# A decoder kernel: values copied out of PSUM by ScalarE, their biases folded into the output bias, and the self blocks' rotated keys and queries rounded by ScalarE

## The reference, cut to what matters

```python
Q = (x @ wq.T + bq); K = (x @ wk.T + bk); V = (x @ wv.T + bv)   # split into 16 heads
Q, K = _rope(Q, K)                                             # only in layer 0's self attention
out = softmax(Q @ K.T / sqrt(8)) @ V                           # by head, then joined
x = layernorm(x + out @ wo.T + bo)
```

## Time and profile before

| | us |
|---|---|
| median of 3 runs | 429.88 (429.31 to 430.05) |
| the profiled execution's own time | 428.95 |
| its span on the core | 427.0 |
| PE busy | 382.7 (90%) |
| DVE busy | 282.6 (66%) |
| ACT busy | 226.1 (53%) |

### The profile page before, as it was taken

How to read it: one execution, slowest core, us unless ns; L and a number is a source line. 1 busy time by engine, 2 the same in 40 slices (tenths; PEclk the granted TensorE clock), 3 DMA queues, 4 the chain that set the end, 5 groups by cost and what they waited for, 6 DMA issues and landing times.

```text
span 427.0 us, 9206 instructions
## 1 busy us (share of the span) xinstructions
PE 382.7 (90%) x3326; PEld 337.5 (79%) x3326; DVE 282.6 (66%) x833; ACT 226.1 (53%) x526; POOL 53.8 (13%) x61
## 2 busy tenths in 40 slices
PE   4679898998989999999978999899999969989991
PEld 3577776886779997989967899778998757768991
DVE  6598889888965557622786355754768688835453
ACT  2145566665665564766347555585465546641241
POOL 7700004900000000000000000000002002010124
PEclk9989999999999999999969999999999989999997
DMA  5655311214240000200020000200011112730301
GB/s 161 192 165 182 112 48 29 74 53 119 94 136 2 2 2 0 76 2 2 2 74 2 2 0 2 67 10 1 2 39 51 38 38 72 226 124 2 110 13 33
DMA packets 22603, 25.15 MB, mean 59 GB/s; under 512 B 3224, under 2 KB 17313, under 8 KB 22560
## 3 DMA queue, kind: packets, MB, share of 16 engines
q1 hardware_dynamic: 21088, 22.95, 18.3%
q0 software_dynamic: 512, 0.97, 0.7%
q10 hardware_dynamic: 960, 0.66, 0.6%
HBM read 17.82 MB, written 6.83 MB: 58 GB/s over the span
## 4 chain that ended last, share of the span: by engine, by line
PE 70%; DVE 18%; issue 5%; DMA 3%; ACT 2%; POOL 0%; SPq 0%; POOLq 0%; ACTq 0%; DVEq 0%
PE bank_D L839 13%; PE bank_C L725 10%; PE bank_D L697 9%; PE bank_A L708 8%; DVE negmax L1225 5%; PE bank_A L855 4%; PE bank_A L857 3%; PE bank_A L856 3%; PE bank_D L623 2%; PE bank_D L681 2%; DVE x_rows L1170 1%; PE bank_D L756 1%; PE bank_A L643 1%; PE bank_A L1540 1%; PE bank_A L767 1%
## 5 line engine op out<-in xcount | busy, mean ns | idle before, releaser
L1225 DVE TENSOR_REDUCE negmax<-bank_D 128x2 f32<-128x512 f32 x192 | 127.4, 684 | 42.2 <-PE bank_D L697 41.9
L985 ACT ACTIVATE expo<-bank_A 128x512 f32<-128x512 f32 x192 | 110.2, 597 | 50.5 <-PE bank_A L708 49.2
L697 PE MATMUL bank_D<-k_head,q_sp 128*128 128x256 f32 x384 | 91.1, 322 | 9.8 <-DVE negmax L1225 5.1
L708 PE MATMUL bank_A<-q_sp,k_head 128*128 128x256 f32 x384 | 82.5, 300 | 4.8 <-DVE q_sp L1220 3.4
L1021 ACT ACTIVATE hidden<-bank_A,b 128x256 f32<-128x256 f32 x128 | 53.7, 471 | 52.1 <-PE bank_A L857 51.9
L697 PEld LDWEIGHTS bank_D<-k_head,q_sp 128*128 128x128 f32 x384 | 61.7, 199 | 22.1 <-issue 10.1
L839 PE MATMUL bank_D<-mix_w,hidden 128*128 128x128 f32 x512 | 67.8, 275 | 0.0
L708 PEld LDWEIGHTS bank_A<-q_sp,k_head 128*128 128x128 f32 x384 | 60.8, 194 | 7.6 <-DVE q_sp L1220 5.0
L839 PEld LDWEIGHTS bank_D<-mix_w,hidden 128*128 128x128 f32 x512 | 62.5, 191 | 1.6 <-issue 1.6
L725 PE MATMUL bank_C<-expo,v_aug 128*32 128x256 f32 x768 | 46.4, 382 | 1.1 <-ACT expo L985 0.8
L1284 DVE SCALAR_TENSOR_TENSOR y_mixture<-bank_D,g_w,y_mixture 128x128 f32<-128x128 f32 x64 | 22.3, 348 | 30.5 <-PE bank_D L839 28.8
(11 more groups left out here) (181 smaller groups left out, 536.4 us busy)
## 6 DMA issues: line engine op xcount, KB each, us to landing
mix_w<-in_mix_w SPq DMA_DIRECT2D x24, 256.0 KB, 3.6
k_head<-k_scratch SPq DMA_DIRECT2D x92, 48.0 KB
k_scratch<-qk_hi SPq DMA_DIRECT2D x24, 128.0 KB, 2.4
w_last<-in_mix_w SPq DMA_DIRECT2D x8, 256.0 KB, 5.7
k_scratch<-qk_lo SPq DMA_DIRECT2D x12, 128.0 KB, 2.4
proj_w<-in_proj SPq DMA_DIRECT2D x1, 640.0 KB, 5.1
xe_scratch<-empty_row SPq DMA_DIRECT2D x1, 520.0 KB, 4.5
expo<-xe_scratch SPq DMA_DIRECT2D x2, 260.0 KB, 3.1
```

The lines of the kernel that those rows point to most:

```text
L697: last = mm(where(seq, b, ("max", k))[:, qt * SEQ:(qt + 1) * SEQ], q_sps[SET[seq, b]][:, k // 4, qt * P:(qt + 1) * P], k_heads[SET[seq, b] ...
L708: last = mm(where(seq, b, ("exp", h))[:, kt * SEQ:(kt + 1) * SEQ], k_heads[SET[seq, b]][:, t, g, kt * P:(kt + 1) * P], q_sps[SET[seq, b]][ ...
L985: activate(expo[:, exp_slot(seq, b, h), :], where(seq, b, ("exp", h))[:], ACT.Exp, scale=float(HD) ** -0.5).then_inc(free(seq, b, ("exp", ...
L1225: V.tensor_reduce(negmaxes[SET[seq, b]][:, s // 4, :, 32 * (s % 4)], where(seq, b, ("max", s))[:].rearrange("p (q n) -> p q n", q=QT), AX. ...
```

## The change

The values' PSUM bank moves from pool D to pool A, and ACT copies the values out by two plain copies, without a bias, in all twelve blocks. The biases of V in layer 0 are folded: in sequence 0's self and cross block PE turns the bias row (step 6, pool A), ACT copies it to `bias_T`, PE multiplies it with the output weights (step 9, pool D), and DVE adds the product to the output bias's row in place. POOL's residual waits until that is done. In self blocks DVE adds the rotated parts (steps -13 and -5), ACT rounds the sum to `qk_hi` in the same steps, and DVE subtracts one step later (-12 and -4).

```diff
-KEYS_AT, KEYS_LOW_AT = -14, -13
-QUERIES_AT, QUERIES_LOW_AT, QUERIES_SPREAD_AT = -6, -5, -3
+KEYS_AT, KEYS_LOW_AT, SELF_KEYS_LOW_AT = -14, -13, -12
+QUERIES_AT, QUERIES_LOW_AT, SELF_QUERIES_LOW_AT, QUERIES_SPREAD_AT = -6, -5, -4, -3
 OWN_VALUES_AT = -4
+FOLD_TURN_AT, FOLD_AT = 6, 9
+FOLDED = {SELF0: ("bv0", "bo0"), CROSS0: ("bvx0", "box0")}
...
             if s == OWN_VALUES_AT:
-                turn(seq, b, "v", "D")
+                turn(seq, b, "v", "A")
+            if s == FOLD_TURN_AT and seq == 0 and b in FOLDED:
+                turn(seq, b, "bias", "A")
+            if s == FOLD_AT and seq == 0 and b in FOLDED:
+                turn(seq, b, "fold", "D")
...
                 def residual(seq, b, bias):
+                    if b in FOLDED:
+                        wait_drained(pool, 0, b, "fold")
...
+                        if s == FOLD_TURN_AT and seq == 0 and b in FOLDED:
...
+                            nc.tensor.transpose(where(seq, b, "bias")[:, 0:P], row(FOLDED[b][0]), ident
+                                                ).then_inc(full(seq, b, "bias"), 1)
+                        if s == FOLD_AT and seq == 0 and b in FOLDED:
+                            wait_drained(pe, seq, b, "bias")
+                            wait_free(pe, seq, b, "fold")
+                            mm(where(seq, b, "fold")[:, 0:P], bias_T[:], weight(wo[b]),
+                               start=True, stop=True).then_inc(full(seq, b, "fold"), 1)
...
+                def round_rotated(seq, b, i, added, ready):
+
+                    act.wait_ge(added, seq + 1)
+                    activate(qk_hi[:, i, :], rope[:, 0, :], ACT.Copy).then_inc(ready, 1)
...
+                def values(seq, b):
+
+                    if (seq, b) in BEFORE:
+                        prior, block_before = BEFORE[seq, b]
+                        act.wait_ge(pair_done, 2 * ORDER[prior, block_before] + 2)
...
+                    wait_filled(act, seq, b, "v")
...
+                        last = activate(v_column(v_augs[SET[seq, b]], odd, 0, HD), src, ACT.Copy)
+                    last.then_inc(free(seq, b, "v"), 1)
...
                 def split(seq, b, what, i, ready):
 
-                    wait_drained(dve, seq, b, what)
-                    link(V.tensor_tensor(rope[:, 0, :], rope[:, 0, :], rope[:, 1, :], ALU.add))
-                    rounded = V.tensor_copy(qk_hi[:, i, :], rope[:, 0, :])
                     if what == "k":
-                        rounded.then_inc(k_high_ready, 1)
                         dve.wait_ge(k_high_ready, seq + 1)
                     else:
-                        link(rounded)
+                        dve.wait_ge(q_high_ready, seq + 1)
                     V.tensor_tensor(qk_lo[:, i, :], rope[:, 0, :], qk_hi[:, i, :].bitcast(f32),
                                     ALU.subtract).then_inc(ready[seq], 1)
```

More of the change, by code:

```diff
@@ L955, in copy_out @@
                              ).then_inc(free(seq, b, what), 1)
+                def values(seq, b):
+                    if (seq, b) in BEFORE:
+                        prior, block_before = BEFORE[seq, b]
+                        act.wait_ge(pair_done, 2 * ORDER[prior, block_before] + 2)
+                    else:
+                        act.wait_ge(dve_cleared, 4 * SETS + 1)
+                    wait_filled(act, seq, b, "v")
+                    for odd in range(2):
+                        src = where(seq, b, "v")[:, 0:QT * P].rearrange(
+                            "p (q a b d) -> p q a b d", q=QT, b=2, d=HD)[:, :, :, odd, :]
+                        last = activate(v_column(v_augs[SET[seq, b]], odd, 0, HD), src, ACT.Copy)
+                    last.then_inc(free(seq, b, "v"), 1)
                 bk = {CROSS0: col("bkx0"), CROSS1: 0.0}
@@ L961, in attention @@
                     for s in ATTENTION_STEPS:
+                        if s == OWN_VALUES_AT:
+                            values(seq, b)
+                        if s == FOLD_TURN_AT and seq == 0 and b in FOLDED:
+                            wait_filled(act, seq, b, "bias")
+                            activate(bias_T[:], where(seq, b, "bias")[:, 0:P], ACT.Copy
+                                     ).then_inc(free(seq, b, "bias"), 1)
                         if s == KEYS_AT and b > SELF0:
@@ L964, in attention @@
                             high(seq, b, "k", 1, bk[b])
+                        if s == KEYS_LOW_AT and b == SELF0:
+                            if (seq, b) in NEXT_TO:
+                                act.wait_ge(k_stored, 16 * KEY_KINDS * ORDER[seq, b])
+                            round_rotated(seq, b, 1, k_added, k_high_ready)
+                        if s == QUERIES_LOW_AT and b == SELF0:
+                            round_rotated(seq, b, 0, q_added, q_high_ready)
                         if s == QUERIES_AT and b > SELF0:
@@ L1086, in _ @@
                 V = nc.vector
-                def values(seq, b, bv):
-                    if b == SELF0:
-                        dve.wait_ge(ld_bv0, 16)
-                    elif bv is not None:
-                        dve.wait_ge(ld_rows, 16)
-                    if (seq, b) in BEFORE:
-                        prior, block_before = BEFORE[seq, b]
-                        dve.wait_ge(pair_done, 2 * ORDER[prior, block_before] + 2)
-                    wait_filled(dve, seq, b, "v")
-                    for odd in range(2):
-                        src = where(seq, b, "v")[:, 0:QT * P].rearrange(
-                            "p (q a b d) -> p q a b d", q=QT, b=2, d=HD)[:, :, :, odd, :]
-                        dst = v_column(v_augs[SET[seq, b]], odd, 0, HD)
-                        if bv is None:
-                            last = V.tensor_copy(dst, src)
-                        else:
-                            bias = row(bv).rearrange("p (a b d) -> p a b d", b=2, d=HD)[:, :, odd, :]
-                            last = V.tensor_tensor(
-                                dst, src, bias.unsqueeze(1).broadcast_to([P, QT, HEADS // 2, HD]), ALU.add)
-                    last.then_inc(free(seq, b, "v"), 1)
                 def low(seq, b, what, i, bias):
@@ L1184, in attention @@
                             rotate(seq, b, "k", "bk0", "bk0s")
-                        if s == KEYS_LOW_AT:
+                        if s == KEYS_LOW_AT and b == SELF0:
+                            add_rotated(seq, b, "k", k_added)
+                        if s == (SELF_KEYS_LOW_AT if b == SELF0 else KEYS_LOW_AT):
                             if (seq, b) in NEXT_TO:
@@ L1191, in attention @@
                                 low(seq, b, "k", 1, bk[b])
-                        if s == OWN_VALUES_AT:
-                            values(seq, b, bv[b])
+                        if s == FOLD_AT and seq == 0 and b in FOLDED:
+                            wait_filled(dve, seq, b, "fold")
+                            dve.wait_ge(ld_rows, 16)
+                            V.tensor_tensor(row(FOLDED[b][1]), where(seq, b, "fold")[:, 0:P],
+                                            row(FOLDED[b][1]), ALU.add
+                                            ).then_inc(free(seq, b, "fold"), 1)
                         if s == QUERIES_AT and b == SELF0:
@@ L1196, in attention @@
                             rotate(seq, b, "q", "bq0", "bq0s")
-                        if s == QUERIES_LOW_AT:
+                        if s == QUERIES_LOW_AT and b == SELF0:
+                            add_rotated(seq, b, "q", q_added)
+                        if s == (SELF_QUERIES_LOW_AT if b == SELF0 else QUERIES_LOW_AT):
                             if b == SELF0:
```

10 lines of the change are left out of this document (9 added, 1 removed).

## The result

The changed kernel takes 432.56 us (median of 8 runs, 431.67 to 435.86), the kernel before 429.44 (8 runs). The ratio is 1.0076, 95% interval 1.0055 to 1.0098: slower by 2.4 to 4.2 us, where no change was forecast (430.3 us, 427.7 to 432.5). The profiled execution took 432.37 us, of which 430.2 are the span.

The account below looks back on a forecast made before the run. PE was taken to bound 120 to 210 us, with PE and DVE near each other from 26 to 120. Terms summed to +0.4 us on the profiled 428.95, giving 429.35, or 430.3 as median; range 427.7 to 432.5 (8 in 10).

Parts of the forecast that it names:

- the term for the PE-bound stretches: Stretches with a mixture beside the attention: nothing, ACT's bursts at worst making PE wait once or twice, +0.1 us (0 to +0.8).
- Start and block 1's keys: First key loads 0.65 us later behind ACT's rounding, 0.67 saved in block 1's key step, first fold 0.28: +0.25 us.
- Query steps of blocks 2 and 5: aT held behind ACT's rounding, product by key 1.0 us late, spread behind the exponential: +0.35 us each.
- Key steps: Blocks 2 and 5: first bank some 0.7 us earlier, but ACT's second exponential held behind the rounding: -0.25 us each.
- Values in cross blocks: Blocks 3 and 4: without the values' turn in pool D the scores start 0.2 us sooner: -0.2 us each.
- Work moved: DVE loses 24 value instructions (6.7 us) and 8 casts (2.7), gains two fold additions: 8.9 us off; ACT gains some 9.
- Sum: All terms: 0.25 + 0.1 + 0.7 - 0.5 - 0.4 + 0.1 + 0.15 (second fold) = +0.4 us.
- ACT's queue becomes the bound: Six later rounding copies wait for DVE ahead of work PE needs: +2.25 us, 432.1 us; chance 0.28.
- DVE's relief reaches the end: From 26 to 120 us DVE loses some 4.0 us, half of it gained: 427.9 us; chance 0.31.
- The clock: New waits at blocks 2 and 5 let the granted clock fall, 1.5 us or so each: 433.3 us; chance 0.08.
- what I said would show it: New profile: rounding behind DVE's addition, PE waits by product by key, longer DVE waits, later loads, short value copies.
- the two signs that I had given for a wrong forecast: PE's waits for DVE in 26 to 120 us shrink by 2 us unreplaced, or waits for ACT grow in mixture stretches.

Follow-up runs that it names:

- experiment 1: Run v_in_d: the changed kernel with the values' turn taken from pool D again, ScalarE still copying them; 430.96 us against 429.83, ratio 1.0029.
- experiment 5: The kernel before with only the values' turn moved from pool D to pool A, DVE still copying them; 434.06 us against 429.20, ratio 1.0104.
- v_in_d: The changed kernel with the values' turn back in pool D, ScalarE still copying; 430.96 us (ratio 1.0029), in a second set 429.49 (0.9994).
- experiments 1, 4, 6: 1: v_in_d. 4: round_only and round_only_first. 6: the changed kernel with ScalarE rounding the self blocks' queries one step later, behind the aT copy; 431.75 us, ratio 1.0055.
- experiment 2: The changed kernel with DVE rounding the self blocks' keys and queries again, values still on ScalarE in pool A, folds kept; 431.66 us, ratio 1.0052.
- round_only: The kernel before with only the self blocks' rounding on ScalarE, DVE's value copies ahead of its subtraction for the queries; 430.28 us against 429.83, ratio 1.0019.
- round_only_first: The kernel before with only the self blocks' rounding on ScalarE, DVE's subtraction for the queries ahead of its value copies; 429.20 us against 429.80, ratio 0.9986.
- keys_only: The kernel before with only the rounding of the keys on ScalarE, queries and values as before; 428.78 us against 429.80, ratio 0.9980.
- v_in_d_keys_only: As v_in_d, but of the self blocks ScalarE rounds only the keys and DVE the queries; 429.13 us against 429.98, ratio 0.9969.
- experiment 7: Both kernels profiled again unchanged (before 428.92 us, changed 431.50), then each with seven more matmuls in a PE wait near the end (before 430.85, changed 432.52).
- v_in_d_no_round: The changed kernel with the values' turn back in pool D and the rounding back on DVE, values on ScalarE, folds kept; 429.83 us against 429.83, ratio 1.0002.
- experiment 9: Runs v_in_d_keys_only and keys_only, in which ScalarE rounds the keys and DVE the queries; ratios 0.9969 and 0.9980.

## Why the prediction was wrong

**The step that failed is the term for the PE-bound stretches,** "I take nothing, with ACT's bursts of 0.5 us at worst making PE wait once or twice: +0.1 (0 to +0.8)". I read the move of the values' turn out of pool D as a relief for pool D, and gave pool A's side only ScalarE's bursts. The turn itself takes one of three banks at each block, and PE waits for the release of an older one, at this turn or up to three turns later. It cost 0.51, 0.38 and 0.39 us, 1.28 in all, in blocks 6, 9 and 10; experiment 1 takes them away with one word, experiment 5 puts them into the kernel before. I had found that effect in the query step (L708 "falls on bank A0") and did not carry it to the later blocks.

From 35 to 366 us the terms of the sum come to +0.05 and the table to 2.1. Of the 2.0 between them the bank's turn is 1.2, the key steps 0.5, the cross blocks with the second fold 0.3 and the query steps 0.2, less 0.2 in block 11.

Point by point, in us, predicted and measured:

- *Start and block 1's keys:* +0.25. Against the trace of before without the fall at 22 us, -1.07 and -1.15 less -1.22, so +0.1; with 0.60 between two traces of v_in_d this is no more than "small". The price that it rests on, 0.65 at the first store, was 0.35 and 0.46 in the two traces, and none of it reached PE: the first scores start at 15.41 and 15.14 us, and in the kernel before at 15.52 and 15.26.
- *Query steps of blocks 2 and 5:* +0.35 twice. Measured +0.48 and +0.46, by the mechanism told: aT behind the rounding, the product by key 1.03 late, the spread behind the exponential. With ScalarE draining the values it takes both edits: with the bank turned back, with the rounding alone or with it behind aT 0.13 to 0.17 are left (experiments 1, 4, 6), with the bank's turn and no rounding nothing (experiment 2). With DVE draining them the turn alone costs 0.5 (experiment 5).
- *Key steps:* -0.25 twice. Block 5 gave -0.21, and so did block 2 in the four traces of round_only, round_only_first, keys_only and v_in_d_keys_only. In the changed kernel block 2 gave +0.19: DVE idles 0.42 us ahead of its first rotation (36.48) for nothing that the profile shows. The same idle time is in all seven traces in which queries and values are both on ScalarE, and in none of the other ten; its cause stays open.
- *Values in cross blocks:* -0.2 twice. Nothing came of it: +0.06 over 55 to 93 us, and +0.17 with the turn in pool D.
- *Work moved:* 8.9 us off DVE predicted, 8.0 measured. The 6.7 us for the values multiply 24 by the duration of one; the earlier trace rows give 3.8 + 1.9 = 5.7 us busy, since the two copies of a pair overlap.
- *Sum:* +0.4 predicted, about 2.1 plus 0.1 at the start by the steps, 2.4 to 4.2 by the runs. The rest, 0.2 to 2 us, is not pinned to the change; the late copy or clock fall at 375 to 383 us and the late load at 403 to 406 (experiment 7) are of that size and differ between traces of one kernel.

**The rivals.** *ACT's queue becomes the bound* named the right side and a time (432.1) near the result, which is luck in good part: its 0.65 at the start was not paid, its query steps were 0.47 each and not 0.65, and it has nothing for the bank's turn in the late blocks. Held aT costs only where the bank is met. *DVE's relief reaches the end* failed: DVE lost the 4.1 us between 26 and 120 us, as predicted, and v_in_d, which keeps 3.4 of it (78.7 us busy) without the bank's turn, is no faster than the kernel before in either set (1.0008 to 1.0050, 0.9973 to 1.0016); v_in_d_no_round keeps 2.0 (80.2 us busy) and is no faster either (0.9988 to 1.0016). The rule of the Trainium skill ("Perfetto Trace Analysis", Optimizing Scalar/DVE Operations), that work moved off a busy DVE may pay, bought nothing here for the change as a whole; the keys' rounding alone gained 0.2 us at each of two places (experiment 9). *The clock*: the wait at L718, 0.54 us, let nothing fall; the granted clock is 1.00 from 22 to 210 us. But the fall at 22 us, which I took as a trait of the kernel before, is in one of its two traces only, and that made the trace of before a poor base for anything ahead of 35 us. Over all seventeen traces it comes in none of the seven that have queries and values both on ScalarE, and in seven of the other ten: whether the change makes it rarer stays open.

Of what I said would show it, the copy to qk_hi behind DVE's addition, the wait ahead of L718 (predicted up to 1.0, seen as 0.54 in each of blocks 2 and 5), the longer waits of DVE for the output projection (0.93 instead of 0.63 in two cross blocks) and copies of values of about 0.3 us (0.44 to 0.46 for two) came true; loads 0.5 to 0.8 later and "by 30 us within 0.5" did not. The lower end of the range, 427.7, is called the relief rival's middle, which is 427.9 by its own sum. And one of the two signs that I had given for a wrong forecast came true: PE waits for ScalarE in the mixture stretches, at blocks 6 and 10.

## What to carry to other kernels

When an edit moves a buffer's turn from one pool to another, walk the new pool's turns at every block, and write down which release each new turn waits for: PE-bound stretches are where such a wait is paid in full. Compare traces by how the offset grows from one fixed event to the next, not by their ends; a second trace of the unchanged kernel tells which stretches can be read at all. Two edits, each free by itself, can meet in one bank: undo them one at a time and together.

## What the runs showed of the hardware that I had not expected

The granted clock falls from 1.00 to 0.50 (2.4 to 1.2 GHz) two to four times in an execution ahead of its idle end. The places move between traces of the same code (13 to 21 or 22 to 26 us; 380 to 384 or none). At 380, where PE is the bound, the traces with a fall lose 1.45 to 1.55 us against the first trace of the kernel before, and some 0.5 against the traces without one. What the fall at 13 to 21 us costs the runs don't show: the trace that lacks it ran at the same speed there.

At 375 to 383 us the first trace of the kernel before stands alone against all sixteen others. Six of them have a clock fall there and lose 1.45 to 1.55 us. The other ten have none and lose 0.97 to 1.07: ScalarE's last copy of a value product starts about 1 us after the product has ended, at the full clock, and PE waits for it. In v_in_d (the product on PE, the copy, PE's next wait):

```profile
379.73 1.93 PE L735 MATMUL bank_C<-expo,v_aug 128*32 128x256 f32 x32
...
382.75 0.38 ACT L1043 ACTIVATE ctx_sb<-bank_C 128x256 f32<-128x256 f32 x1 [3.08 <-PE bank_C L735]
...
383.19 0.66 PE L749 MATMUL bank_D<-const,ctx_sb 128*128 128x128 f32 x4 [0.67 <-ACT ctx_sb L1043]
```

The product ends at 381.66 and the copy starts at 382.75. Nothing in the profile accounts for it. Which of the two comes is a matter of the execution: the changed kernel's first trace has the fall, its second the late copy. The first execution of the kernel before had neither, and still took as long as the second, which had the fall (428.95 and 428.92 us): the second had been 1.22 us earlier at 35 us.
